# An alignment stage in a six-stage kernel: lane-edge copies on ScalarE, choice flags over all rows at once, the distance matrix reloaded tile by tile

## What is computed

```
def _pairwise_euclidean(a, b):
    aa = jnp.sum(a * a, axis=-1)[:, None]; bb = jnp.sum(b * b, axis=-1)[None, :]
    return jnp.sqrt(jnp.maximum(aa + bb - 2.0 * a @ b.T, 0.0))
# R: cost of the best path to each cell
    r = d_ij + jnp.minimum(jnp.minimum(up, left), diag)
# the way back from the last cell, at each step
    choice = jnp.argmin(jnp.stack([cd, cu, cl]))       # diagonal, up, left
    ni = jnp.where(choice <= 1, i - 1, i)
    nj = jnp.where((choice == 0) | (choice == 2), j - 1, j)
# result
    contrib = small[i_idx] * valid[:, None]
    expanded = jnp.zeros((T_large, d)).at[j_idx].add(contrib)
...
x = x + _L1_xattn_ref(ctx_1024, _layernorm(x, axis=-1))
```

## Time and profile before

| | |
|---|---|
| median of 3 runs | 2059.95 us |
| lowest and highest of them | 2052.17 and 2061.83 us |
| the profiled execution, time | 2054.18 us |
| its span in the profile | 2052.4 us |
| TensorE, VectorE, ScalarE, GpSimd busy | 86%, 56%, 31%, 39% |
| the alignment stage, in the span | 1433 to 1612 us |

### The profile page before, as it was taken

How to read it: one execution, slowest core, us unless ns; L and a number is a source line. 1 busy time by engine, 2 the same in 40 slices (tenths; PEclk the granted TensorE clock), 3 DMA queues, 4 the chain that set the end, 5 groups by cost and what they waited for, 6 DMA issues and landing times.

```text
span 2052.4 us, 22616 instructions
## 1 busy us (share of the span) xinstructions
PE 1755.7 (86%) x8406; PEld 844.9 (41%) x8422; DVE 1150.0 (56%) x1631; ACT 642.4 (31%) x1072; POOL 791.0 (39%) x439
## 2 busy tenths in 40 slices
PE   7888877978999999999998659999603989789998
PEld 4666654432332333323335334444401457534443
DVE  3444443198999999999983332222397364531211
ACT  2333332334554555555541311111300140111211
POOL 1343332008998999999982110000130014000000
PEclk8999996988999999999997669999655679779999
DMA  2111101011000000000005000100350100101110
GB/s 69 31 31 36 31 16 49 3 55 48 10 10 24 10 11 24 10 15 21 9 6 220 2 0 16 46 31 15 71 137 0 31 0 1 42 0 42 41 41 20
DMA packets 34896, 65.50 MB, mean 32 GB/s; under 512 B 12692, under 2 KB 21800, under 8 KB 33140
## 3 DMA queue, kind: packets, MB, share of 16 engines
q1 hardware_dynamic: 34820, 64.49, 10.5%
HBM read 55.80 MB, written 8.67 MB: 31 GB/s over the span
## 4 chain that ended last, share of the span: by engine, by line
PE 52%; POOL 19%; DVE 15%; issue 11%; ACT 2%; DMA 1%; SPq 0%; DVEq 0%; ACTq 0%; POOLq 0%
POOL arena L1006 18%; PE ps L1222 6%; PE ps L1982 5%; PE ps L1994 5%; PE ps L198 4%; PE ps L1235 3%; PE ps L339 3%; PE ps L344 3%; PE ps L221 2%; DVE arena L934 2%; PE ps L357 2%; DVE arena L474 2%; PE ps L1757 2%; PE ps L1773 1%; PE ps L214 1%
## 5 line engine op out<-in xcount | busy, mean ns | idle before, releaser
L1006 POOL TENSOR_TENSOR arena<-arena 128x1024 f32<-128x1024 f32 x248 | 577.9, 2401 | 24.0 <-DVE arena L960 17.7
L787 PE MATMUL ps<-arena 32*128 32x512 f32 x2016 | 471.9, 640 | 24.5 <-DVE arena L941 19.3
L892 ACT ACTIVATE arena<-arena 128x1024 f32<-128x1024 f32 x248 | 262.2, 1057 | 294.2 <-DVE arena L950 294.2
L963 DVE TENSOR_TENSOR arena<-arena,ps 128x1024 f32<-128x1024 f32 x248 | 302.4, 1220 | 9.9 <-POOL arena L1006 8.7
L950 DVE TENSOR_TENSOR arena<-arena,ps 128x1024 f32<-128x1024 f32 x248 | 301.1, 1214 | 8.1 <-PE ps L787 8.1
L787 PEld LDWEIGHTS ps<-arena 32*128 32x128 f32 x2016 | 163.2, 188 | 334.6 <-issue 141.0
L2052 DVE TENSOR_TENSOR arena<-arena,ps 128x512 f32<-128x512 f32 x64 | 44.0, 688 | 183.0 <-ACT arena L2027 183.0
L811 PE MATMUL ps<-arena 128*32 128x512 f32 x1024 | 139.6, 617 | 5.2 <-DVE arena L963 3.1
L1222 PE MATMUL ps<-arena 128*128 128x512 f32 x288 | 131.0, 600 | 5.9 <-DVE arena L1093 5.9
L1982 PE MATMUL ps<-arena 128*128 128x512 f32 x256 | 116.8, 600 | 0.0
L1994 PE MATMUL ps<-arena 128*128 128x512 f32 x256 | 112.3, 592 | 0.0
(11 more groups left out here) (266 smaller groups left out, 2266.9 us busy)
## 6 DMA issues: line engine op xcount, KB each, us to landing
arena<-ctxT SPq DMA_DIRECT2D x32, 257.0 KB, 3.1
arena<-ctxT SPq DMA_DIRECT2D x8, 1028.0 KB, 14.5
arena<-L_ffn_w SPq DMA_DIRECT2D x16, 512.0 KB, 4.2
arena<-ctx_rows SPq DMA_DIRECT2D x8, 960.0 KB
m_rows<-arena SPq DMA_DIRECT2D x16, 256.0 KB, 2.7
arena<-m_rows SPq DMA_DIRECT2D x64, 64.0 KB
arena<-L_ffn_eW SPq DMA_DIRECT2D x8, 512.0 KB, 3.6
m_yd<-arena SPq DMA_DIRECT2D x64, 32.0 KB
```

The costliest lines, as they stand in the source:

```text
L787: mm = nc.tensor.matmul(ps[:, ring(n) + jj, :], weights[r], m_row[r, buf, t % CH, :], start=True, stop=True)
L892: nc.scalar.activation(m_xa[:, u, t % 2], m_xa[:, u, t % 2], ACT.Exp, scale=-1.0).then_inc(S["m_dec"], 1)
L963: nc.vector.tensor_tensor(m_h[:, u, t % 2], m_xa[:, u, t % 2], ps[:, ring(n):ring(n) + 2, :], ALU.add).then_inc(S["m_use"], 1)
L1006: nc.gpsimd.tensor_tensor(m_xa[:, u, t % 2], m_xa[:, u, t % 2], m_h[:, u, (t - 1) % 2], ALU.mult).then_inc(S["m_kept"], 1)
```

## The change

Four things change, all in the alignment stage.

1. **The reload by tile.** SP stores tile g, then reloads tile g-1, with three DMAs of 4 partitions each, as soon as that tile's store has landed; 24 reloads in place of 3. Stores signal two semaphores in turn. `d_D` moves to a place that is free while the distances are still being made.
2. **Edge copies on ScalarE.** In the forward loop the copy from lane 0 to lane 1 goes to ScalarE, which waits for the scan of the step before; the one from lane 1 to 2 stays. On the way back both casts go to ScalarE. VectorE's scans wait for ScalarE's semaphores (`d_least`, `d_choice`).
3. **Flags in five operations.** The chunks, `d_stay` and all of GpSimd's and ScalarE's part in them are gone. Behind the forward loop five VectorE operations go over all 34 slots (96x34x86) and four copies over all edges.
4. **The transposed rows by three.** ScalarE takes PSUM out in 10 pieces of three rows and one of four, between its edge copies; TensorE uses the four banks in turn and waits for `d_mev` before it starts on one again.

```diff
-        CHUNKS = ((0, 7), (7, 14), (14, 21), (21, 27), (27, SLOTS))
-        TURNED = (25, 16, 7, 0)
+        PER = 3
+        LAST = (SLOTS - 1) // PER - 1
...
+            def back(g):
+                sp.wait_ge(*S.at(f"d_out{g % 2}", 16 * (g // 2) + 16))
+                for k in range(SEG):
+                    r = slice(B * k + SL * g, B * k + SL * g + SL)
+                    sp.dma_start(d_D[r, k:k + L].rearrange("p j i -> p (j i)"),
+                                 dist[k, g * P:(g + 1) * P].rearrange("(b j) i -> b (j i)", j=L)).then_inc(S["d_back"], 16)
+            keep(0)
+            for g in range(1, TT):
+                keep(g)
+                back(g - 1)
+            back(TT - 1)
...
+            for s in range(SLOTS):
+                act.wait_ge(*S.at("d_fwd", max(3 * s, 1)))
+                nc.scalar.copy(d_least[lane(1), s, 0:1], d_R[lane(0), s, W:WW]).then_inc(S["d_least"], 1)
...
+            for n in range(SLOTS - 1):
+                act.wait_ge(*S.at("d_v", n + 1))
+                for k in range(SEG - 1):
+                    nc.scalar.copy(d_E[lane(k), 0:1], d_V[lane(k + 1), SLOTS - 1 - n, W:WW]).then_inc(S["d_choice"], 1)
+                if n >= 4 and n % PER == 1:
+                    turned(n - 4, PER)
+            turned(SLOTS - 4, 4)
...
+            ch.step(nc.vector.tensor_tensor(dg[:, :, W:0:-1], R[:, 0:SLOTS, 0:W], R[:, 0:SLOTS, own], ALU.is_le))
+            ch.link(nc.vector.tensor_tensor(least[:, :, own], R[:, 1:SLOTS + 1, 0:W], least[:, :, own], ALU.subtract))
+            ch.link(nc.vector.scalar_tensor_tensor(out=up[:, :, own], in0=dg[:, :, own], scalar=-TINY,
+                                                   in1=least[:, :, W:0:-1], op0=ALU.mult, op1=ALU.is_ge))
+            ch.step(nc.vector.scalar_tensor_tensor(out=lf[:, :, own], in0=dg[:, :, own], scalar=0.0,
+                                                   in1=up[:, :, own], op0=ALU.is_equal, op1=ALU.is_gt))
+            ch.sync()
+            ch.link(nc.vector.tensor_tensor(dg[:, :, own], dg[:, :, own], up[:, :, own], ALU.is_gt))
```

More of the change, by code:

```diff
@@ L1411, in build, with turned_to @@
         ACT_SQ = 5
[L1412 to L1413 removed]
         TINY = 1e-30
[L1415 removed]
+        PER = 3
+        LAST = (SLOTS - 1) // PER - 1
+        def turned_to(n):
+            e = min(n // PER, LAST)
+            return e, (SLOTS - 1 if e == LAST else PER * e + PER - 1) - n
         def lane(k):
@@ L1420, in d_load, with keep @@
         def d_load(sp):
-            for g in range(TT):
+            def keep(g):
                 sp.wait_ge(*S.at("d_sqrt", 2 * g + 2))
[L1423 to L1427, removed]
+                sp.dma_start(dist[:, g * P:(g + 1) * P].rearrange("k p i -> p k i"), d_dt[g]).then_inc(S[f"d_out{g % 2}"], 16)
+            def back(g):
[9 more added lines that the diff above has]
+            back(TT - 1)
             sp.wait_ge(*S.at("d_ab", TT))
@@ L1470, in d_pe @@
                 s = SLOTS - 1 - n
-                t = n // 9
+                e, o = turned_to(n)
+                if e >= 4 and o == (3 if e == LAST else PER - 1):
+                    pe.wait_ge(*S.at("d_mev", e - 3))
                 pe.wait_ge(*S.at("d_v", n + 1))
-                nc.tensor.transpose(ps[0:W, t, :].bitcast(BF16)[:, (s - TURNED[t]) * PB:(s - TURNED[t] + 1) * PB],
+                nc.tensor.transpose(ps[0:W, e % 4, :].bitcast(BF16)[:, o * PB:o * PB + PB],
                                     d_V[0:PB, s, 1:WW], identb[0:PB, 0:PB]).then_inc(S["d_vT"], 1)
@@ L1495, in expand @@
                 mm.then_inc(S["d_exp"], 1)
-            pe.wait_ge(*S.at("d_mev", len(TURNED)))
+            pe.wait_ge(*S.at("d_mev", SLOTS // PER))
             expand(0)
@@ L1633, in d_dve @@
+            ch.sync()
+            ch.link(nc.vector.tensor_tensor(dg[:, :, own], dg[:, :, own], up[:, :, own], ALU.is_gt))
+            for k in range(SEG - 1):
+                for v in (1, 2):
+                    ch.step(nc.vector.tensor_copy(by_lane(v, k)[:, 0:SLOTS - 1, 0:1], by_lane(v, k + 1)[:, 1:SLOTS, W:WW]))
+            ch.sync()
             for n in range(SLOTS):
                 s = SLOTS - 1 - n
-                if s == a + 1:
-                    dve.wait_ge(*S.at("d_choice", NC))
-                    edges(0, a)
+                if n:
+                    dve.wait_ge(*S.at("d_choice", 2 * n))
```

82 lines of the change are left out of this document (20 added, 62 removed).

## The result

The changed kernel takes 2039.52 us (median of 5 runs, 2037.49 to 2044.59), the kernel before 2055.32 (5 runs of the same session, 2052.17 to 2061.83): a ratio of 0.9919, 95% interval 0.99 to 0.9938. The profiled execution took 2038.24 us, 15.9 less than the profiled one of before. The forecast was 2042.6.

The account below looks back on a forecast made before the run. The prediction took the alignment stage as a single chain, mostly VectorE's work, with nearly ten us of DMA alone before it. Reload +9.6 and VectorE's road -21.2 gave -11.6 on the profiled 2054.18: 2042.6 us, range 2029 to 2061.

Parts of the forecast that it names:

- VectorE's road: VectorE's work in the alignment stage: shorter by 8.8 (forward loop and flags) + 12.2 (way back) + 0.2 (last piece) = 21.2 us.
- The forward step: Forward loop, scan to scan: 1.00 us falls to 0.825 as one edge copy leaves VectorE; the loop 28.15 us.
- The fifth: Last of the five flag operations, bf16 throughout: taken at 3.23 us; at twice the rate, five cost 14.7 instead of 16.3.
- The way back: Loop behind the flags: step falls from 1.37 to 1.02 us as two casts leave VectorE; gain 12.2 us.
- ScalarE's cover: ScalarE's edge copies hidden behind VectorE's work between scans: 0.485 us forward, 0.68 on the way back, at most 0.49 needed there.
- The reload: Loading distances back before the forward loop: 24 small loads at 1.0 us each land at 1493, 9.6 us later than before.
- The forecast's queue: Reload, from 1465: 24 loads of 1.0 us on the same four engines, six stores of 0.5, 1 us until landing is seen.
- What else SP issues is behind them: Claim that the context rows, issued after the reload, still take 45 us and are needed 80 us behind the landing.
- rival (4): Reload: SP awaits stores queued behind older reloads; if the queue runs dry, 7.85 us a tile, 2078 us in all; chance 0.05.
- Rival (3): Reload: four adjacent partitions take 1.75 us a load, engines in step; +27.6 - 21.2, 2060.6 us; chance 0.24.
- (1): Reload: the small loads keep up with the tiles; -2.5 - 21.2, 2030.5 us; chance 0.13.
- (2): Reload: loads go at the rate of earlier four-partition loads, 0.78 us each; +4.3 - 21.2, 2037.3 us; chance 0.20.

Follow-up runs that it names:

- x_vcast: x_oldload with the way back's two casts across lanes returned to VectorE; stage 164.58 us against 153.17, run 2042.78 us.
- x_twice: x_oldload with each ScalarE copy across lanes done twice, the first into a cell nothing reads; stage 154.50 us, run 2036.72 us.
- x_tailalone: x_tail with the context rows' loads held back until the reload has landed; wait for the distances 16.48 us, run 2047.5 us.
- x_lag: Changed kernel with each tile's three small loads only after the store of three tiles later is issued; wait 14.78 us, run 2042.45 us.
- x_tail: Changed kernel with all eight stores first, then the same twenty-four small loads; wait for the distances 26.64 us, run 2056.71 us.
- x_laghold: x_lag with the context rows held back until the reload has landed; wait for the distances 11.59 us, run 2041.48 us.
- r_after: The changed kernel itself run once more, no edit; median 2044.64 us of 7 runs, ratio 0.9918 to the kernel before, stage 162.19 us.
- x_best: x_oldload with context rows held until the reload landed and the last two flag operations swapped, the last a plain tensor_tensor; 2027.03 us, ratio 0.9857 to the kernel before.
- x_quarters: x_tailalone with each row loaded as four pieces, the last number of each left out; wait 18.99 us, run 2041.29 us.
- x_oldload: Changed kernel with the old reload, three loads of 32 partitions after all eight stores; stage 153.17 us, run 2039.53 us, ratio 0.9915 to the kernel before.

## Why the prediction was right

**VectorE's road, -21.2 forecast, -22.8 measured.** The forward step is 0.83 (0.825), the loop 28.4 us (28.15). The first four flags are 3.20 us each (3.23). The fifth is 1.5 of the 1.6 us of difference: I took 3.23 for it, with twice the rate as the bound, and it runs at twice the rate, 1.70. The way back gained 12.15 (12.2), the last piece 0.24 (0.2), and x_vcast shows that 11.4 of the way back's gain are the two casts. ScalarE's cover held; only in the first step does VectorE stand still for it, from 1490.41 to 1490.56, as the 0.1 us from the earlier trace rows had it. The price of 0.21 us for each of the two copies was right, they take 0.40 together. x_twice says with what margin: two more copies a step make the step 0.04 us longer.

**The reload, +9.6 forecast, +8.3 measured.** The forecast's queue lasts 28 us, 24 x 1.0 for the loads, 3 for stores and 1 for the landing; from the first issue to the landing it took 28.1. The 1.3 us are its start: 1461.82, which is 1463.67 in the time of the kernel before, and not 1465. That the length fits is in good part luck. The 1.0 us was put between two rows without a reason that fixed it, and the runs show what it was made of: 0.70 us when nothing else moves (x_tailalone), 0.94 to 1.17 beside stores, context rows or both (x_lag, x_tail, the changed kernel). So the load by itself was priced too high, and what stands beside it too low. That each reload has four engines, and the same four, is borne out by the packet records: never more than four rows at once in x_laghold, four at once with a brief fifth in x_tailalone. Two sentences failed. "What else SP issues is behind them" priced the context rows at nothing: holding them back is worth 3.2 us of VectorE's wait from x_lag to x_laghold and 10.2 from x_tail to x_tailalone. And rival (4)'s mechanism, SyncE standing at a store's landing before it goes on, is in the chain of waits four times, and three times the next store stands behind it; I had given it 0.05 and thought it all or nothing. The last store goes out 6.3 us later than in x_lag, counted from L250, and 2 to 3 us of that show in VectorE's wait; the rest, as I read it, is hidden by a queue that is backed up anyway.

**Rival (3)**, 1.75 us a load, did not happen. The Trainium skill (SBUF — State Buffer, Door 1: The DMA port swizzle) had four adjacent partitions at 27.6 GB/s. In x_tailalone such loads, three lanes by turns at the same place of each, move 68 GB/s over 14.5 us; the measurement speaks against the rule as I used it, for all twenty-four. Early on something like it is seen: from 1484.5 to 1487 the loads move 40 GB/s at a share of 0.22, from 1490 to 1496 they move 93 at 0.24, and a row takes up to 1.4 us at first and 0.42 later. That fits the forecast's own sentence that an engine which gets ahead loosens the jam, but which partitions each engine was writing isn't recorded, so it is not shown.

**Rivals (1) and (2).** (1) fell, the loads did not keep up. (2), 0.78 us each, from the 57 GB/s of the earlier trace rows, was nearer to the load by itself (0.70) than the forecast was; with the traffic beside it the load came to more.

**The total.** The reload cost 1.3 us less than forecast and the flags gained 1.6 more, 2.9 together; 1.5 more lie outside the stage. Profiled 2038.24 against 2042.6. The forecast's sign and its range held. That a whole run came so near it is chance as well: the same kernel's other profiled execution, r_after, took 2048.28 us, 10 more, with 0.8 of them in the stage.

## What to carry to other kernels

Cutting a transfer by partitions to overlap it did not pay here, by eighths or by halves: three loads of 32 rows took 6.0 to 6.4 us behind the last store, twenty-four of 4 rows took 17 to 28 from the first issue and made the stores among them about twice as late. A cut in which each piece keeps all 32 partitions was not tried. The reload by tile gave back 8.3 us of the 22.8 that the rest of the change had gained. Look in the chain of waits for a store that has grown longer: a store took 2.6 to 3.0 us with no load ahead of it and 4.9 to 7.4 with loads. And when a change of some us is judged, compare the stage between two untouched instructions, since behind the stage this program moved by 5 us from one profiled execution to another, and ahead of it by up to 19.

## What the runs showed of the hardware

- A `tensor_tensor` of 96x2924 with all operands bf16 takes 1.70 us, in place or not (x_best); a `scalar_tensor_tensor` of the same shape and types, not in place, 3.20.
- ScalarE copies of 32x1 last 0.19 us; the next began 0.21 us after one that signals a semaphore (the changed kernel) and 0.10 after one that signals none (x_twice).
- DMA loads of 4 rows of 11 KB, with many queued and nothing else moving, keep the DMA engines 0.21 busy over 14.5 us at 68 GB/s (x_tailalone), and no more than four rows, for 0.1 us five, move at once. With each row cut into four pieces it is still four to six pieces (x_quarters).
- Issuing one load of 4 rows takes SyncE 0.29 us, with four pieces a row 0.60.
- Behind the alignment TensorE's clock is at 0.5, and the first 18 us of the next stage ran at 0.59 or at 0.71 of full speed with the same work, 4.6 us apart at the program's end (the changed kernel and x_oldload).
